# Last attention of a gated cross-attention network: maximum tiles as eight 64x32 matmuls, with the fourth score of a step between the two tiles

## The reference, cut to what matters

```python
qkv = (x @ W_qkv).reshape(Bx, Nx, 3, H, D)
...
logits = jnp.einsum('bqhd,bkhd->bhqk', q * scale, k)
def masked_attn(tok_mask):
    key_mask = jnp.concatenate([jnp.ones((Bx, REG), bool), tok_mask], axis=1)
    l = jnp.where(key_mask[:, None, None, :], logits, -jnp.inf)
    a = jax.nn.softmax(l, axis=-1)
    return jnp.einsum('bhqk,bkhd->bqhd', a, v)
x_pos = masked_attn(pos)
x_neg = masked_attn(~pos)
...
return out @ W_proj + b_proj
```

## Time and profile before

| | |
|---|---|
| median of three runs | 1279.92 us |
| the profiled execution | 1277.68 us |
| its span, first to last instruction | 1275.6 us |
| TensorE busy | 1195.5 us (94%) |
| VectorE busy | 973.4 us (76%) |
| ScalarE busy | 818.6 us (64%) |
| units 0 to 14 of the last attention (240 steps) | 598.4 to 1209.5 us of the span |
| unit 15, without tiles | 1209.5 to 1253 us |

### The profile page before, as it was taken

One profiled execution on the slowest core, in us unless ns is written; L12 is line 12 of the kernel. 1 busy time (PEld: TensorE's weight loads), 2 busy tenths in 40 slices (PEclk: granted clock), 3 DMA queues, 4 the chain that ended last, 5 costly groups with the idle time before them and its releaser, 6 DMA issues.

```text
span 1275.6 us, 26127 instructions
## 1 busy us (share of the span) xinstructions
PE 1195.5 (94%) x10370; PEld 549.2 (43%) x10370; DVE 973.4 (76%) x1431; ACT 818.6 (64%) x1471; POOL 257.4 (20%) x200
## 2 busy tenths in 40 slices
PE   4888997999999899988999999999999999999998
PEld 2566784555558446444233323232332323232345
DVE  4896586565536758667999999999999999999912
ACT  1324564577761563213888888888888888888872
POOL 2130443455661242370000000000000000000000
PEclk8879996799999999998999999999999999999999
DMA  6100227456510234453255443554345443555014
GB/s 197 28 1 1 38 60 124 79 118 127 89 39 1 72 130 126 131 70 53 57 88 94 68 95 64 100 101 74 82 81 95 89 83 72 99 87 87 12 41 138
DMA packets 89960, 101.71 MB, mean 80 GB/s; under 512 B 22122, under 2 KB 60268, under 8 KB 89840
## 3 DMA queue, kind: packets, MB, share of 16 engines
q1 hardware_dynamic: 89840, 100.06, 38.7%
HBM read 71.47 MB, written 24.33 MB: 75 GB/s over the span
## 4 chain that ended last, share of the span: by engine, by line
PE 59%; DVE 30%; ACT 3%; issue 2%; SPq 2%; DMA 1%; POOL 1%; POOLq 0%; DVEq 0%; ACTq 0%
DVE sm L2187 23%; PE ps L1658 10%; PE ps L1649 9%; PE ps L1636 7%; PE ps L1425 3%; PE ps L1519 2%; PE ps L1416 2%; PE ps L1417 2%; PE ps L1719 2%; PE ps L1478 2%; PE ps L1381 1%; PE ps L1383 1%; PE ps L1434 1%; PE ps L1539 1%; DVE XN L1795 1%
## 5 line engine op out<-in xcount | busy, mean ns | idle before, releaser
L2187 DVE TENSOR_REDUCE sm<-ps 128x1 f32<-128x1024 f32 x512 | 602.0, 1219 | 34.0 <-PE ps L1636 29.9
L1127 ACT ACTIVATE W<-ps 128x512 f32<-128x512 f32 x1024 | 535.0, 604 | 123.4 <-PE ps L1658 121.0
L1658 PE MATMUL ps<-R 99*32 99x512 bf16 x4096 | 317.5, 384 | 0.9
L1649 PE MATMUL ps<-W,R 128*32 128x512 f32 x2048 | 265.4, 594 | 0.0
L1658 PEld LDWEIGHTS ps<-R 99*32 99x32 bf16 x4096 | 85.1, 94 | 203.6 <-ACT W L1127 156.3
L1636 PE MATMUL ps<-R 50*128 50x512 bf16 x512 | 91.0, 390 | 12.6 <-DVE sm L2187 8.3
L1050 ACT ACTIVATE R<-ps 77x512 f32<-77x512 f32 x128 | 75.2, 592 | 32.2 <-PE ps L1417 24.2
L1636 PE MATMUL ps<-KM,R 50*128 50x512 bf16 x512 | 88.7, 384 | 5.2 <-DVE sm L2187 0.2
L878 POOL COPY R<-R 128x512 f32<-128x512 f32 x16 | 9.7, 611 | 385.5 <-PE ps L1649 385.5
L1649 PEld LDWEIGHTS ps<-W,R 128*32 128x32 f32 x2048 | 62.9, 111 | 45.8 <-issue 0.5
L1960 DVE TENSOR_REDUCE small<-ps 128x4 bf16<-128x308 f32 x128 | 57.4, 473 | 24.0 <-PE ps L1383 23.9
(11 more groups left out here) (259 smaller groups left out, 1506.4 us busy)
## 6 DMA issues: line engine op xcount, KB each, us to landing
R<-x_parts SPq DMA_DIRECT2D x96, 128.0 KB, 4.8
R<-q_parts SPq DMA_DIRECT2D x192, 64.0 KB
R<-q_parts SPq DMA_DIRECT2D x96, 128.0 KB
R<-k_parts SPq DMA_DIRECT2D x96, 128.0 KB
x_parts<-R SPq DMA_DIRECT2D x8, 768.0 KB, 5.6
q_parts<-R SPq DMA_DIRECT2D x24, 256.0 KB, 2.6
k_parts<-R SPq DMA_DIRECT2D x24, 256.0 KB, 2.6
X<-in_x SPq DMA_DIRECT2D x4, 1024.0 KB, 10.3
```

The source lines that it names most:

```text
L1127: act.activation(PR[:, s % 2, h, :], third_bank("score", 64 * u + n), ACT.Exp, scale=0.25).then_inc(s_sfree, 1)
L1649: mm = pe.matmul(bank(7)[32 * h:32 * h + 32, :], VST[j][:, k, h, :], PR[:, s % 2, h, :], start=(k == 0), stop=(k == TB - 1))
L1658: mm = pe.matmul(o[32 * c:32 * c + 32, :], KST[j][0:MAX_ROW + 1, h, t:t + 32], QST[j][0:MAX_ROW + 1, h, 512 * (s // 8):512 * (s // 8) + 51 ...
L2187: dve.tensor_reduce(MX[:, half, h, q:q + 1], bank(2 * ((p + 1) % 2), 2), AX, ALU.max).then_inc(s_tfree, 1)
```

## The change

A tile is made of eight matmuls of 32 weight columns (two for each quarter of the output partitions) in place of two of 128 columns. The first tile of a step comes before the fourth score instead of after it, the second tile stays after it. So that the users of the three banks keep their order, the rows turns move from the first tile of a step to the second.

```diff
         PLAN = [[("tile", n)] for n in range(32)]
-        PLAN[2].insert(0, ("rows", 1))
-        PLAN[18].insert(0, ("rows", 0))
+        PLAN[3].insert(0, ("rows", 1))
+        PLAN[19].insert(0, ("rows", 0))
         PLAN_LAST = [[] for _ in range(32)]
-        PLAN_LAST[2].append(("rows", 1))
+        PLAN_LAST[3].append(("rows", 1))
...
                 q, h = a // 4, a % 4
-                for i in range(2):
-                    v = slice(64 * i, 64 * i + MROWS)
-                    mm = pe.matmul(pl[:, 512 * i:512 * i + 512], QMH[j][h][v, P * q:P * q + P], KM[j][v, h, :],
-                                   start=True, stop=True)
+                for c in range(4):
+                    t = P * q + 32 * c
+                    for i in range(2):
+                        v = slice(64 * i, 64 * i + MROWS)
+                        mm = pe.matmul(pl[32 * c:32 * c + 32, 512 * i:512 * i + 512], QMH[j][h][v, t:t + 32],
+                                       KM[j][v, h, :], start=True, stop=True)
                 mm.then_inc(s_turn, 1)
...
                         values2(us, s - 1, js)
+                    turns(plan[2 * n])
                     scores2(us, s, 3, js)
-                    turns(plan[2 * n])
                     turns(plan[2 * n + 1])
```

## The result

The changed kernel takes **1313.39 us** (median of four runs, 1312.72 to 1315.5) against 1279.85 for the kernel before on the same chips: the ratio is 1.0271, with a 95% interval of 1.0256 to 1.0287. It is slower by 2.7%, 33.5 us. The profiled execution took 1312.93 us with a span of 1311.1.

A forecast was written before the change was run, and what follows sets the result against it. TensorE and VectorE were taken to pass the wait back and forth, in 2.546 us steps. Steps averaging 2.71 add 39 us over 240 steps to the profiled 1277.68: 1317 us, range 1264 to 1328.

The forecast's parts named there:

- the likeliest one: Every passage in the steps of units 0 to 14 is paid: 1300 to 1328 us, chance 0.66.
- The passages: On TensorE, each change of matmul shape around a 64-row, 32-column tile costs 0.10 us, four per step instead of two.
- free: Rival: on TensorE the passage costs nothing at 32 columns; 1269 us, or 1255; chance 0.24.
- half free: Rival: one direction of the passage on TensorE costs nothing, the other 0.10 us; 1293 us; chance 0.06.
- Eight matmuls at once in 0.24: On TensorE a tile's eight matmuls run at once, in 0.24 us instead of 0.22.
- two rounds: Rival: a tile's eight matmuls run as two rounds of four, adding 0.20 us per tile; 1395 us; chance 0.04.
- TensorE's own need of 2.61: Scores, values, both tiles and four passages take TensorE alone 2.61 us per step.
- The round that was to set the step, 2.68: From one third score to the next, through values, tile A, fourth score and its exponential: 2.68 us, over TensorE's 2.61.
- the 0.11 from the end of a score: Term of the round: from the fourth score's end to its exponential on an idle ScalarE, 0.11 us.
- The rows turn, 2.90: In one step of eight the second score waits for the fourth exponential, 0.22 us earlier: 2.90 us.
- The sum: Average step in units 0 to 14 of 2.71 us against 2.546, over 240 steps: +39 us.

The follow-up runs named there:

- the pair of 64 and 65 rows: Changed kernel, its steps' tiles made from the score stacks in four matmuls, keys 0 to 511 only, contracting 64 or 65 rows: 1312.90 and 1272.79 us.
- the move alone: Changed kernel with the old tile shape, two matmuls of 128 columns, still one tile on each side of the fourth score: 1312.04 us, ratio 1.0266.

## Why the prediction was right, and where a step of it failed

The forecast was 1317 us, in a range from 1264 to 1328; 1313.4 was measured, and the case that came about is the likeliest one.

- **The passages** (0.10 each, four per step): right, and shown by the pair of 64 and 65 rows. What the prologue's rows showed at 64 and 128 columns carried over to 32 columns. So the rivals "free" and "half free" fall.
- **Eight matmuls at once in 0.24:** right; a tile with its passage takes 0.34 to 0.35. The rival "two rounds" falls, and so does the floor of about 25 ns between starts in "TensorE: Matmul & The Clock Gate", Part 1, of the Trainium skill for matmuls like these: the eight of a tile started within some 0.02 us.
- **TensorE's own need of 2.61:** 2.63 measured, and the plain step is no longer than that.
- **The round that was to set the step, 2.68: this step failed in its size.** The wait that it names is there in the plain steps (0.31 ahead of the load at 814.52), but the matmul behind that load starts 0.22 after the second score's, where it would have started anyway. The term mis-sized is the 0.11 from the end of a score to the exponential on an idle ScalarE. The fourth score ended at 816.46 and its exponential started at 816.51 (next fence), so it is 0.05. The 0.11 came from the first exponential of a step. With 0.05 the round is 2.62, level with TensorE. The trace of the kernel before could have told: of its exponentials on an idle ScalarE nearly all are first ones of a step, at 0.11, but the few others, such as the second one in the last two lines of the fence, start 0.05 after their score (592.58 to 592.63, at a granted clock of 0.50, where the first ones take 0.11 all the same). In the code the first exponential of a step waits for one semaphore more than the others, the one that frees its set of `PR`. Whether that is the 0.06 between them was not tried.

```profile
816.51 0.60 ACT L1127 ACTIVATE W<-ps 128x512 f32<-128x512 f32 x1 [0.33 <-PE ps L1660]
...
591.96 0.62 PE L1658 MATMUL ps<-R 99*32 99x512 bf16 x4
592.63 0.60 ACT L1127 ACTIVATE W<-ps 128x512 f32<-128x512 f32 x1 [0.47 <-PE ps L1658]
```

- **The rows turn, 2.90: this step failed in its mechanism.** The prediction let VectorE's negations hide in its slack and had the second score wait for ScalarE. In truth it is the third score that waits, for the negation, which stands behind tile A's reduce on VectorE's queue; 3.14 measured. Putting the turn ahead of tile A removed the wait (2.84).
- **The sum:** +39 us forecast for the stretch, +36.9 measured. Of every eight steps six came out 0.05 smaller, the one with a copy of bank 7 took 2.69, and the turn's step was 0.24 larger. The misses nearly cancelled: (6 x 2.63 + 2.69 + 3.14) / 8 = 2.70 against 2.71. That the sum is this close is luck; that it lies in the range is not, since either miss alone would have left it there (an average of 2.67 or 2.74, some 1308 or 1324 us).

The hope behind such a change is not wrong in itself: the waits for a reduce did go. But they had cost only 0.14 us in an average plain step (2.51, against 2.37 without a wait). In their place two further passages cost 0.20 and the rest 2.63 - 2.37 - 0.20 = 0.06, of which the narrow tiles are 0.02 (2.61 with the move alone). So the 179 plain steps grew from 2.51 to 2.63, 21 us in all. The 30 steps with a copy took 2.69 before and after. The 30 steps with a turn grew from 2.59 to 3.14, another 16 us: these few steps make over two fifths of the loss, and 9 of their 16 us are the negation behind the reduce.

## What to carry to other kernels

Before small matmuls are put between others, find in the trace what a passage between their shapes costs: take the distance of the starts across the passage and subtract the distance inside a run of one shape. Here a tile of 50 or 64 rows beside matmuls of 99 or 128 pays 0.10 us at each end, so such tiles belong together in one run. Where TensorE has no time to spare, splitting a run to spare a wait pays only if the wait is longer than two passages, averaged over the steps. When an operation moves past another on TensorE, look also at the order in which the engine behind it works its list: a short negation behind a long reduce held a bank and made the step 0.30 us longer.

## What was not expected of the hardware

- The step between 64 and 65 rows is sharp: 2.62 us and 2.40 us for the same step, 1312.9 and 1272.8 us for the kernel.
- An idle ScalarE started the fourth exponential 0.05 us after the recorded end of its matmuls (in 210 steps of the changed kernel), but the first one of a step 0.11 after the earlier trace rows (in 223 steps of the kernel before).
- Eight matmuls of 50 rows by 32 columns run at once as well as four of 99 rows by 32 do: 0.41 us from the first start to the last end, against 0.40.
